# Two more units of an attention kernel turn their probabilities by transposing DMA, and the page copies are cut and moved

## The reference, cut to what matters

```
x = x + einsum('bsi,boi->bso', x, weight[adapter_ids])
q, k, v = x @ Wq.T, x @ Wk.T, x @ Wv.T            # heads of 128: 32 for q, 8 for k and v
q, k = rope(rmsnorm(q)), rope(rmsnorm(k))
kc = k_cache[block_table].reshape(8, 512, 8, 128) # 16 pages of 32 rows for each batch
vc = v_cache[block_table].reshape(8, 512, 8, 128)
k_all, v_all = concat([kc, k], 1), concat([vc, v], 1)
scores = einsum('bqhd,bkhd->bhqk', q, k_all) * SCALE, masked by cache_seqlens
o = einsum('bhqk,bkhd->bqhd', softmax(scores), v_all)
x = x + o.reshape(8, 128, 4096) @ Wo.T
```

## Time and profile before

| | us |
|---|---|
| median of 3 runs | 1015.48 (1013.26 to 1015.71) |
| the profiled execution | 1014.77 |
| its span | 1013.0 |
| TensorE matmuls busy | 1000.4 (99%) |
| weight loads of TensorE | 870.9 (86%) |
| VectorE busy | 852.1 (84%) |
| ScalarE busy | 799.4 (79%) |
| GpSimd busy | 784.6 (77%) |

### The profile page before, as it was taken

One profiled execution on the slowest core, in us unless ns is written; L12 is line 12 of the kernel. 1 busy time (PEld: TensorE's weight loads), 2 busy tenths in 40 slices (PEclk: granted clock), 3 DMA queues, 4 the chain that ended last, 5 costly groups with the idle time before them and its releaser, 6 DMA issues.

```text
span 1013.0 us, 19440 instructions
## 1 busy us (share of the span) xinstructions
PE 1000.4 (99%) x5551; PEld 870.9 (86%) x5551; DVE 852.1 (84%) x1782; ACT 799.4 (79%) x2093; POOL 784.6 (77%) x803
## 2 busy tenths in 40 slices
PE   8999999999999999999999999999999999999998
PEld 5778888888888888888888888888888888888887
DVE  7676667666898899899999999989998999988995
ACT  4554555656798899888888988898898888988884
POOL 4986767574698889897898888898798978888672
DMA  8888979997788888888889898888889888898873
GB/s 259 246 256 267 296 189 259 220 229 212 139 156 166 153 161 157 156 163 157 161 158 162 160 161 154 154 169 155 163 152 172 154 147 169 160 165 140 154 147 86
DMA packets 465740, 179.51 MB, mean 177 GB/s; under 512 B 408529, under 2 KB 445794, under 8 KB 463586
## 3 DMA queue, kind: packets, MB, share of 16 engines
q1 hardware_dynamic: 359424, 148.84, 71.7%
q10 hardware_dynamic: 105186, 27.33, 12.5%
q0 software_dynamic: 1024, 2.10, 0.7%
HBM read 109.25 MB, written 35.66 MB: 143 GB/s over the span
## 4 chain that ended last, share of the span: by engine, by line
PE 93%; DVE 2%; SPq 2%; DMA 2%; issue 1%; ACT 1%; ACTq 0%; DVEq 0%
PE S L1387 21%; PE O L1320 7%; PE O L1322 7%; PE O L1321 7%; PE Q L1322 6%; PE Q L1320 6%; PE Y L1320 6%; PE Q L1321 6%; PE Y L1321 6%; PE Y L1322 6%; PE T L1326 5%; PE KV L1321 3%; PE KV L1320 3%; PE KV L1322 3%; PE KV L1340 1%; SPq L320 1%
## 5 line engine op out<-in xcount | busy, mean ns | idle before, releaser
L1061 DVE SCALAR_TENSOR_TENSOR pr<-pr,rc,raw 128x640 f16<-128x640 f32 x204 | 238.8, 1170 | 14.9 <-ACT raw L802 8.3
L1033 DVE CUSTOM_DVE_ANT_0 pr<-S,mask,rst 128x640 f32<-128x640 f32 x256 | 225.5, 881 | 21.1 <-PE S L1387 18.8
L822 ACT ACTIVATE pr<-pr,nb 128x640 f32<-128x640 f32 x256 | 211.8, 827 | 21.9 <-DVE nb L1033 21.8
L597 POOL TENSOR_TENSOR m<-m 128x512 f32<-128x512 f32 x63 | 110.3, 1750 | 77.3 <-DVE m L1100 74.4
L802 ACT ACTIVATE raw<-pr,rc 128x640 f16<-128x640 f32 x204 | 163.4, 826 | 0.6 <-DVE rc L1049 0.3
L550 POOL TENSOR_TENSOR kl<-raw,kh 128x512 fp32r<-128x512 f32 x64 | 97.1, 1517 | 46.4 <-ACT kh L700 45.6
L1387 PE MATMUL S<-kh,qh 128*128 128x320 f32 x512 | 120.9, 317 | 3.5 <-DVE nb L1033 3.4
L1387 PE MATMUL S<-kh,ql 128*128 128x320 f32 x512 | 116.6, 309 | 0.0
L571 POOL TENSOR_SCALAR ptl<-first 128x512 fp32r<-128x512 f16 x130 | 103.6, 797 | 16.8 <-issue 6.0
L1387 PE MATMUL S<-kl,qh 128*128 128x320 f32 x512 | 116.2, 308 | 0.3 <-POOL kl L550 0.3
L1387 PEld LDWEIGHTS S<-kh,qh 128*128 128x128 f32 x512 | 91.7, 189 | 23.7 <-issue 4.6
(11 more groups left out here) (177 smaller groups left out, 2710.9 us busy)
## 6 DMA issues: line engine op xcount, KB each, us to landing
cache_rows<-in_kv SPq DMA_DIRECT2D x80, 256.0 KB, 4.9
wraw<-in_wall SPq DMA_DIRECT2D x74, 256.0 KB, 4.4
raw<-cache_rows SPq DMA_DIRECT2D x63, 256.0 KB, 3.9
raw<-cache_rows ACTq DMA_DIRECT2D x49, 256.0 KB, 5.0
cache_rows<-in_kv ACTq DMA_DIRECT2D x48, 256.0 KB, 4.9
mask<-mask_rows SPq DMA_DIRECT2D x64, 128.0 KB, 4.0
first<-in_lw SPq DMA_DIRECT2D x5, 1024.0 KB, 7.4
acc<-in_x SPq DMA_DIRECT2D x8, 256.0 KB, 7.9
```

What stands on the lines that cost most here:

```text
L597: e.tensor_tensor(m1[:, :, :], m1[:, :, :], m2[:, :, :], ALU.add).then_inc(q_added, 1)
L822: e.activation(pr[:, slot(u, g), :], pr[:, slot(u, g), :], ACT.Exp, bias=nb[:, u % 2, g:g + 1], scale=-1.0, accum_out=sm[:, u % 2, g:g + 1 ...
L1033: e.tensor_tensor_reduce(pr[:, slot(u, g), :].rearrange("p (a n) -> p a n", a=2), S[:, :, 0:320], mask[:, u % 2, :].rearrange("p (a n) -> ...
L1061: e.scalar_tensor_tensor(out=lower16(u, g), in0=pr[:, slot(u, g), :], scalar=rc[:, u % 2, g:g + 1], in1=upper16[:, g, :], op0=ALU.mult, op ...
```

## The change

NA goes from 12 to 10: units 10 and 11 are turned by transposing transfers. The copies are spread over the periods in another way, and a copy leaves out the rows of the first key head, which nobody reads from `cache_rows`: 14 rows, 224 KB. Each row of 16 KB is moved as 16 slices of 1 KB, the slices outermost. On SyncE the copies of a period are now issued ahead of the values' load (`load_v`), or the first two groups of them where there are three. `copy_page` is one function for both queues.

```
-NA = 12
+NA = 10
-COPY_SP = (0, 1, 1, 1, 0, 1, 2, 3, 3, 3, 3, 2)
-COPY_ACT = (1, 2, 2, 2, 2, 2, 1, 0, 0, 0, 0, 0)
+COPY_SP = (0, 1, 1, 1, 1, 1, 2, 3, 3, 3, 0, 1, 0)
+COPY_ACT = (2, 2, 2, 2, 2, 2, 2, 1, 0, 0, 0, 0, 0)
...
+        def copy_page(e, b, k, number):
+
+            e.dma_start(copy[2:, b, k, :].rearrange("r (s n) -> s r n", s=16),
+                        kv[2:, bass.ds(number, 1), :].rearrange("r a (s n) -> (a s) r n", s=16)
+                        ).then_inc(d_copy[b], 16)
...
                 for j in range(4):
-                    e.dma_start(
-                        copy[:, b, 4 * t + j, :],
-                        kv[:, bass.ds(numbers[j], 1), :].rearrange("r a n -> (r a) n")
-                    ).then_inc(d_copy[b], 16)
+                    copy_page(e, b, 4 * t + j, numbers[j])
...
                 else:
                     load_k(e, i + 2)
-                if NL <= i + 2 < NA:
+                for n, (b, t) in enumerate(copies_of(i)):
+                    if n == 2 and NL <= i + 2 < NA:
+                        load_v(i + 2)
+                    copy_pages(b, t)
+                if len(copies_of(i)) <= 2 and NL <= i + 2 < NA:
                     load_v(i + 2)
-                for b, t in copies_of(i):
-                    copy_pages(b, t)
...
-            def copy_page(b, k, number):
-                e.dma_start(copy[:, b, k, :],
-                            kv[:, bass.ds(number, 1), :].rearrange("r a n -> (r a) n")
-                            ).then_inc(d_copy[b], 16)
...
                 for place in copied[0:2]:
-                    copy_page(*place)
+                    copy_page(e, *place)
```

## The result

| | before | after |
|---|---|---|
| median of 7 runs | 1015.66 (1013.26 to 1017.21) | 1010.27 (1007.61 to 1012.59) |
| the profiled execution | 1014.77 | 1010.72 |
| its span | 1013.0 | 1008.9 |

The ratio is 0.9941, with a 95% interval of 0.9926 to 0.9956: the kernel became faster by 0.59%. The forecast was 1011.0 and "faster".

What follows compares the result with a forecast made beforehand. TensorE's matmuls were taken to bound the kernel, with DMA transfers the tight side. Two units' transposes gave -4.40 us, change-over, copies and issues 0: median 1015.48 to 1011.1, forecast 1011.0 us, range 1008.5 to 1015.

Steps and rivals of the forecast that it cites:

- Two units leave TensorE, 4.40 us: Units 10 and 11 drop 20 transposes each from TensorE, 2.20 us a unit, 4.40 us gained.
- The change-over moves at no cost: Change-over moves from period 12 to 10 with the same instructions and order; periods stay 17.50 and 14.08 us, no difference.
- A copy costs 0.86 us: DMA time of one sliced 224 KB copy: 0.86 us, the bytes' share of today's 0.985, between 0.53 and 1.04.
- rival C: Page copies: if today's large row distances slow them, sliced copies cost about 0.68 us; at most 1 us better.
- Bytes by period, and 1.1 us of lateness in periods 6 and 7: DMA in periods 6 and 7: 17.9 us of work in 16.72, 1.1 us late each, gone by period 8's end.
- one of the signs that the prediction named for being wrong: Signs: TensorE wait between 141 and 208 us; successive ScalarE issues of 2 us or more; change-over costing over 0.8 us.
- About 6 us of slack at the weight chunk of period 8: Second load of period 8's pair to TensorE: slack about 2.9 + 3.3 us, so 2.2 us of lateness costs nothing.
- Rival A: Transfers of periods 6 to 8 run 8 us late against 6 of slack: 1013 to 1014.4 us; chance 0.20.
- Rival B: Sliced copies too slow for periods 0 to 9, slower from 1.14 us a copy; about 1026 at 1.2; chance 0.10.
- Issues cost nothing: Moved copy issues on SyncE and ScalarE, some 0.5 us each: price 0, upper bound two more stops, 3.3 us.
- The sum: Whole kernel: -4.40 us, profiled execution 1014.77 to 1010.4, median 1015.48 to 1011.1, forecast 1011.0.
- its 0.10 for "slower": Whole kernel: chance 0.10 of becoming slower, against 0.68 faster by over 0.3% and 0.22 within.

Runs made afterwards that it cites:

- set 2: One chip: kernel before 1019.43 us, changed kernel again 1011.36; changed kernel with 14 whole rows 1026.13, 16 rows in slices 1022.66, NA = 12 1016.22.
- the 16 sliced rows: Changed kernel copying all 16 rows in slices of 1 KB, 256 KB: 1022.66 us in set 2, 1023.1 in set 3.
- whole rows: Changed kernel with the old copy, 16 rows in pieces of 16 KB: 1016.38 us in set 1, 1022.55 in set 3.
- set 3: One chip: kernel before 1019.08 us; changed kernel with values' load ahead of copies 1011.87, NA = 8 and copies spread 1017.07, 16 whole rows 1022.55, 16 sliced 1023.1.
- the old order: Changed kernel with SyncE issuing the values' load ahead of a period's copies, as before: 1011.87 us, ratio to before 0.9927.
- set 1: One chip: kernel before 1015.99 us; before with only NA = 10 1026.41, only the sliced copy 1016.01; changed kernel with 16 whole rows 1016.38, NA = 8 1017.38.
- the units alone: Kernel before with NA = 10 and nothing else, old copies, schedule and order: 1026.41 us, ratio to before 1.0106.
- the copies alone: Kernel before with only the new copies, 14 rows in 16 slices, old schedule and order, NA = 12: 1016.01 us, ratio to before 0.9997.

## Why the prediction was right, step by step

- **Two units leave TensorE, 4.40 us.** Right to the hundredth in the periods' lengths (16.72 against 14.52), and 4.86 with the next point in set 2.
- **The change-over moves at no cost.** Its price was mis-sized by 0.5 us on the good side. The step said that the same instructions in the same order stand two periods earlier. The weight chunks don't move with it: their slots hang on the period. Period 10 lasts 17.00 us, not 17.50; period 11 has its 14.06 as forecast.
- **A copy costs 0.86 us.** 0.80 by the records of this profile, 0.86 by those of set 2. The Trainium skill's rule on row pitches ("DMA: Bandwidth & Descriptors", section "Latency and other measured facts"), which would have given an estimate of 0.68, isn't borne out here: by the records a piece of 16 KB costs 0.84 us with 2 MB between the rows, and 14 slices that share a row cost 0.80 to 0.86 (rival C). The size of the pieces changed with the distance, so the two are not told apart.
- **Bytes by period, and 1.1 us of lateness in periods 6 and 7.** The shares of 0.93 and 0.97 are as tight as the step said, and no TensorE wait followed in this profile. In that of set 2 there is one, 0.9 us at 169.80 for GpSimd, and period 7 lasts 17.80: one of the signs that the prediction named for being wrong. The new copies in the old tables have such a wait too (0.6 us at 169.83), so it does not need the re-spacing; its cause is open. SyncE issues the pair of period 8 3.1 us later in the period than before; the step had 2.2.
- **About 6 us of slack at the weight chunk of period 8.** The weak step, though near in size. It paired the landing of the second load with the rounding of the first: by the tables (HI_ACT) the first chunk of the pair is rounded in period 8, the second in period 9. The first landed at 185.34 and was rounded at 188.98, which leaves 3.6 us, not 2.9. In the changed kernel the pair lands at 188.8 and 189.6, one of them not before 189; relative to the period 2.4 to 2.5 us later than before, since it is issued later, and 1.1 us ahead of its rounding at 189.92. From ScalarE's wait to TensorE's the step had 3.3 us; the 16 sliced rows give 8.6 - 4.8 = 3.8. So the slack before is 3.6 + 3.8 = 7.4 us. But the step looked at one chunk only. That of period 6 is tighter: in the trace of before it was issued at 145.31, landed at 154.17 (8.9 us) and was rounded at 155.51, which leaves 1.3 us (rows below). With whole rows ScalarE came to it 6.1 us later in the period than in before, and TensorE stood still for 2.3, so again 3.8 us are forgiven: together 5.1 us, and that is where whole rows stop.
- **Rival A, late transfers: 1013 to 1014.4 at 1.04 us a copy.** It didn't occur, but the 16 sliced rows are this rival with 0.97 us a copy, and they gave 1022.66 and 1023.1, some 11 us over the changed kernel. The path was the one described (the pair of period 8, ScalarE, GpSimd, TensorE), the condition was a little too strict, and the price was too low by a factor of three to nearly six. Two things were left out. Lateness was counted only as bytes inside periods 6 to 8, while SyncE's queue carries it over from period to period, masks and weight chunks included: on the third chip the first chunk of the pair lands 12.3 us later in its period than before, not 8, and 10.4 us of that is a later issue; and the change-over behind it stops as well (period 11 lasts 17.26 us instead of 14.06). And a stop was priced at its own length, while the granted clock falls behind it: period 9 lasts 23.84 us for a wait of 4.8. With whole rows in set 3 TensorE's waits from 130 to 300 us are 7.6 us, and the mean granted clock of 0.995 over 1018.8 us is another 5 as an estimate. (That is more than the 8.5 us by which this span exceeds that of the old order in the same set; 0.7 us of waits stand in both, and the periods from 12 on last 14.46 us here and 14.52 there. Why they are shorter is open.)
- **Rival B, the copies too slow from 1.14 us a copy on, by the balance of all early periods.** Too lenient: kernels slower than before appear at 0.82 to 0.97 us a copy, and their stops follow late issues of single loads, which a balance of bytes over ten periods doesn't hold.
- **Issues cost nothing.** Right in time. ScalarE has one issue over 1.2 us between 100 and 210 us (1.56), before had two (2.02 and 2.10). On SyncE single issues of copies took 6.72, 5.26 and 4.92 us in periods 6 to 8, and the step didn't look for them.

The sum also holds nothing that the new copies and tables give by themselves. That was right in set 1, where the new copies alone gave 0.0 us. In set 2 the changed kernel is 8.1 us faster than before, and 3.2 of these stand outside the sum.

Part of the hit was luck. The forecast stood nearer to an edge than its 0.10 for "slower" said: two rows more in a copy, or the same rows in whole pieces, and the changed kernel is 0.3 to 0.7% slower than before on two of the chips.

The chunk of period 6 in the kernel before (SyncE's weight loads from 141 to 150 us, and ScalarE's timeline):

```profile
L412 SPq DMA_DIRECT2D wraw<-in_wall x1: 425/425/425, 145.3 to 145.3; - x1
...
DMA to landing us min/median/max: 8.9/8.9/8.9
```

```profile
155.51 0.64 ACT L700 ACTIVATE wh<-wraw 128x512 fp32r<-128x512 f32 x1
```

## What to carry to other kernels

When a change moves work between engines and also re-spaces the transfers that clear the way, try the parts alone: here the units alone lost 10 us, the copies alone brought nothing, and with the new tables they gained 5 together. Look for the tightest consumer of a queue in every period from which transfers are moved, not in one, and take its slack from issue, landing and use; SyncE's issue time of a small load shows at once how far a queue is behind. A copy whose row count 16 doesn't divide is worth cutting into slices, if there are bytes to be saved by it: it then runs on all 16 rings, and its issue is shorter.

## What the runs showed of the hardware

- After TensorE stood still for 2.3 to 7.5 us its granted clock fell to 0.5 (1.2 GHz) or a mix of the two levels for some microseconds: 0.63 over 4.6 us, 0.50 over 4.2 us, 0.85 and 0.88 over two whole periods. In the changed kernel, whose longest wait behind the start is 1.1 us, it is 1.00 in every window above.
- A VectorE instruction of 0.88 us took 1.39 beside a GpSimd instruction of 1.30 us on other buffers that had started before it. In the kernel with NA = 8 and spread copies the same VectorE instruction started 0.08 us ahead of such a GpSimd one: it took 0.87, and GpSimd's took 1.95.
- An issue can hold its engine: a copy's issue takes 0.55 us on SyncE as a rule, and one took 6.72 in period 6 of the changed kernel, at a DMA share of 0.93; the kernel before has one of 5.74.
- A copy of 14 whole rows has two packets of 4 bytes fewer than one of 16 whole rows, and takes 0.77 us to issue instead of 0.49 on SyncE.
- The same kernel before took 1015.99, 1019.43 and 1019.08 us on three occasions. Kernels with late transfers varied most (1017.41 to 1028.08 in set 3), the changed one least in set 2 (1010.76 to 1011.89), though 1007.61 to 1012.59 at first.
